# A hybrid eight-layer network on one Trainium2 core: one product for values and sums in the head attention, sums, shifts and router moved into neighbouring stages, random-feature results taken one trip later

## The reference

```python
    x = x + _L0_attn_a_ref(_layernorm(x, axis=-1), ...)
    x = x + _L0_ffn_ref(_layernorm(x, axis=-1), ...)
    x = x + _L0_attn_b_ref(_layernorm(x, axis=-1), ...)
    x = x + _L0_ffn_ref(_layernorm(x, axis=-1), ...)
    x = x + _L1_attn_a_ref(_layernorm(x, axis=-1), ...)
    x = x + _L1_ffn_ref(_layernorm(x, axis=-1), ...)
    x = x + _L1_attn_b_ref(_layernorm(x, axis=-1), ...)
    x = x + _L1_ffn_ref(_layernorm(x, axis=-1), ...)
```

```python
        scores = jnp.einsum('bhid,bhjd->bhij', q, k) * scale
        attn = jax.nn.softmax(scores, axis=-1)
        out = jnp.einsum('bhij,bhjd->bhid', attn, v)
```

```python
            t1, t2 = jnp.split(t, 2, axis=-1)
            t2 = jnp.pad(t2, ((0, 0), (1, 0), (0, 0)))[:, :-1]
            return jnp.concatenate([t1, t2], axis=-1)
```

## Time and profile before

| | us |
|---|---|
| median of 3 runs | 6315.28 |
| lowest, highest run | 6312.53, 6316.73 |
| the profiled execution, as timed | 6308.24 |
| its span in the trace | 6306.2 |

### The profile page before, as it was taken

How to read it: one execution, slowest core, us unless ns; L and a number is a source line. 1 busy time by engine, 2 the same in 40 slices (tenths; PEclk the granted TensorE clock), 3 DMA queues, 4 the chain that set the end, 5 groups by cost and what they waited for, 6 DMA issues and landing times. The chain is left out here.

```text
span 6306.2 us, 119595 instructions
## 1 busy us (share of the span) xinstructions
PE 5418.4 (86%) x42357; PEld 2908.8 (46%) x42357; DVE 3589.7 (57%) x4103; ACT 3331.1 (53%) x4993; POOL 2512.4 (40%) x1721
## 2 busy tenths in 40 slices
PE   6876888888887998998898998999897999776998
PEld 2432555555544553564344554554343444343443
DVE  4557999999954554554344554554454343554344
ACT  4555888888854553554444554454343333443343
POOL 1223999999933651652122661662221000000000
PEclk8996999999998999999899999999899999998999
DMA  1002111101011110110000110110000210001121
GB/s 41 1 0 77 31 32 30 33 30 33 29 47 29 40 40 14 41 41 13 1 0 18 45 40 12 42 40 20 28 0 8 54 40 13 0 0 27 32 36 27
DMA packets 136966, 171.03 MB, mean 27 GB/s; under 512 B 32352, under 2 KB 85728, under 8 KB 135520
## 3 DMA queue, kind: packets, MB, share of 16 engines
q1 hardware_dynamic: 136800, 168.85, 10.2%
HBM read 80.11 MB, written 12.85 MB: 15 GB/s over the span
## 5 line engine op out<-in xcount | busy, mean ns | idle before, releaser
L2318 POOL TENSOR_TENSOR arena<-arena,wbig 128x1024 f32<-128x1024 f32 x512 | 1191.8, 2515 | 103.5 <-DMA wbig<-scratch_b 100.3
L2305 DVE TENSOR_TENSOR_SCAN arena<-banks,arena 128x1024 f32<-128x1024 f32 x512 | 1141.5, 2279 | 63.7 <-ACT banks L2249 45.5
L944 ACT ACTIVATE arena<-banks,wbig 128x512 f32<-128x512 f32 x512 | 352.0, 688 | 584.3 <-PE banks L907 572.7
L601 DVE TENSOR_REDUCE arena<-banks 128x4 f32<-128x1024 f32 (+1 forms) x384 | 401.9, 1047 | 432.8 <-PE banks L435 305.1
L957 DVE TENSOR_TENSOR arena<-arena 128x512 f32<-128x512 f32 x512 | 353.3, 692 | 490.2 <-ACT arena L944 434.7
L768 POOL TENSOR_TENSOR X<-X,Z 128x1536 f32<-128x1536 f32 x2 | 9.5, 4758 | 1482.6 <-ACTq L761 1482.6
L1462 POOL TENSOR_TENSOR arena<-arena 128x512 f32<-128x512 f32 x256 | 355.5, 1389 | 594.5 <-DMA arena<-arena 594.5
L2249 ACT ACTIVATE banks<-banks 128x1020 f32<-128x1020 f32 x512 | 518.2, 1012 | 104.3 <-PE banks L2170 96.8
L2254 ACT COPY arena<-banks 128x1024 f32<-128x1024 f32 x512 | 520.8, 1017 | 51.4 <-POOL arena L2318 30.8
L547 ACT ACTIVATE Y<-banks 128x2048 f32<-128x2048 f32 x192 | 305.8, 1593 | 408.4 <-PE banks L471 311.4
L907 PE MATMUL banks<-Z,wbig 128*128 x1024 | 462.2, 597 | 34.3 <-ACTq L56 34.3
(11 more groups left out here) (289 smaller groups left out, 10428.3 us busy)
## 6 DMA issues: line engine op xcount, KB each, us to landing
arena<-arena SPq DMA_DIRECT2D x1024, 64.0 KB, 2.0
arena<-scratch_g SPq DMA_DIRECT2D x32, 1024.0 KB, 13.8
wbig<-scratch_d SPq DMA_DIRECT2D x512, 16.0 KB, 1.7
wbig<-scratch_b SPq DMA_DIRECT2D x64, 128.0 KB, 2.2
wbig<-scratch_c SPq DMA_DIRECT2D x64, 128.0 KB, 2.1
arena<-Z SPq DMA_DIRECT2D x64, 128.0 KB, 2.1
wbig<-in_l_ffn SPq DMA_DIRECT2D x1, 4197.0 KB, 12.9
X<-in_x SPq DMA_DIRECT2D x2, 2048.0 KB, 14.7
```

The source lines that it names most:

```text
L601: dve.tensor_reduce(to, mbank[:, :, :, 0:keys], AX_X, ALU.max).then_inc(dve_m.sem, 1)
L944: act.activation(hid[e % 2][:, f, :], hbank[f], ACT.Relu, bias=b1[:, e, f:f + 1])\
L2305: dve.tensor_tensor_scan(own, line(decay_bank[n % 2]), own, 0.0, ALU.mult, ALU.add)\
L2318: pool.tensor_tensor(four(h[par][:, m * 1024:m * 1024 + 1024]), four(us[n % 2]), Bs[par].unsqueeze(1).to_broadcast([128, 4, SEQ]), ALU.mult)\
```

## The change

**Head attention.** The values of a slot now stand beside eight columns of ones in `vm`, so that one product gives value rows and sum rows; slots are told apart by column half and by which half of `obank` they go to. L488 and its 128x32 weights are gone. As sums now lie eight partitions below their values, DVE copies the whole bank to `raw`, ACT takes logarithm and exponential over 128x512 (with a scale and a bias that make value rows 1), SP moves the reciprocals up by eight partitions with one transfer, and DVE multiplies twice 128x256 into two arrays, of which the output stage takes two products. `qb` and `km` have two buffers. The addition of the values' bias is gone: a small stage puts it through the output weights once.

```diff
                     pe.wait_ge(pool_s.sem, pool_s.at(i, "vm"))
-                    pe.wait_ge(dve_o.sem, dve_o.before(i, last_out))
+                    pe.wait_ge(dve_o.sem, dve_o.at(i, "raw"))
                 for u in range(2):
                     j = 2 * jj + u
                     for g in range(4):
-                        pe.matmul(obank[rows(g), first:SEQ], vm[par][:, c, j, rows(g)], prob[s % 2][:, g, u, first:SEQ],
-                                  start=(s == 0 and u == 0), stop=True, skip_group_check=True)
-                    for g in range(4):
-                        last = pe.matmul(obank[rows(g), SEQ + first:2 * SEQ], k.c["slot_ones"][:, rows(j)],
-                                         prob[s % 2][:, g, u, first:SEQ], start=False, stop=True,
+                        last = pe.matmul(obank[rows(g), jj * SEQ + first:(jj + 1) * SEQ], vm[par][:, c, j, rows(g)],
+                                         prob[s % 2][:, g, u, first:SEQ], start=(s == 0 and u == 0), stop=True,
                                          skip_group_check=True)
                 last.then_inc(pe_s.sem, 1)
...
+            def logarithm(b):
+                act.wait_ge(dve_o.sem, dve_o.at(b + 1, "raw"))
+                act.wait_ge(dve_o.sem, dve_o.at(b, "out"))
+                act.activation(recip, raw, ACT.Ln, scale=k.c["sum_row"], bias=k.c["head_row"]).then_inc(act_s.sem, 1)
+
             def reciprocal(b):
-                act.wait_ge(pe_s.sem, pe_s.at(b + 1, "late"))
-                act.wait_ge(dve_o.sem, dve_o.before(b, "out"))
-                act.activation(recip, obank[:, SEQ:2 * SEQ], ACT.Ln).then_inc(act_s.sem, 1)
                 act.wait_ge(act_s.sem, act_s.at(b + 1, "ln"))
                 act.activation(recip, recip, ACT.Exp, scale=-1.0).then_inc(act_s.sem, 1)
...
+            def heads_raw(b):
+                dve.wait_ge(pe_s.sem, pe_s.at(b + 1, "late"))
+                dve.wait_ge(dve_o.sem, dve_o.at(b, "out"))
+                dve.tensor_copy(raw, obank).then_inc(dve_o.sem, 1)
+
             def heads_out(b):
-                dve.wait_ge(act_s.sem, act_s.at(b + 1, "recip"))
-                to = out[:, bass.ds(b * SEQ, SEQ)]
-                dve.tensor_tensor(to, obank[:, 0:SEQ], recip, ALU.mult).then_inc(dve_o.sem, 1)
-                if bv is not None:
-                    dve.wait_ge(dve_o.sem, dve_o.at(b, "out"))
-                    dve.tensor_scalar(to, to, bv, None, ALU.add).then_inc(dve_o.sem, 1)
-
+                dve.wait_ge(moved.sem, moved.at(b * 16 + 16))
+                for jj in range(2):
+                    part = slice(jj * SEQ, (jj + 1) * SEQ)
+                    last = dve.tensor_tensor(outs[jj][:, bass.ds(b * SEQ, SEQ)], raw[:, part], moved_to[:, part],
+                                             ALU.mult)
+                last.then_inc(dve_o.sem, 1)
...
+            def trip(b, more):
+                if more:
+                    reduce(b + 1, 0)
+                heads_raw(b - 1)
+                if more:
+                    for n in range(1, 8):
+                        reduce(b + 1, n)
+                heads_out(b - 1)
...
+            def trip(b, par, first=False):
+                keys, queries = kk[:, bass.ds(b * SEQ, SEQ)], q[:, bass.ds(b * SEQ, SEQ)]
+                if not first:
+                    pool.wait_ge(pe_m.sem, pe_m.before(b - 1, "m7"))
+                pool.tensor_copy(qb[par], queries).then_inc(pool_s.sem, 1)
+                pool.tensor_tensor(km[par], spread(keys), mask, ALU.mult).then_inc(pool_s.sem, 1)
+                pool.wait_ge(pe_s.sem, pe_s.before(b, "late"))
...
+        @block.sync
+        def _(sp):
+            for b in range(BATCH):
+                sp.wait_ge(act_s.sem, act_s.at(b + 1, "recip"))
+                sp.wait_ge(dve_o.sem, dve_o.at(b, "out"))
+                sp.dma_start(moved_to[0:128 - HEAD_DIM, :], recip[HEAD_DIM:128, :]).then_inc(moved.sem, 16)
```

```diff
+                if dst is add_to:
+                    dve_s.skip(dve, i, "both")
+                else:
+                    dve.tensor_tensor(dst[:, tok(i, TILE)], dst[:, tok(i, TILE)], add_to[:, tok(i, TILE)], ALU.add)\
+                        .then_inc(dve_s.sem, 1)
...
+        if shifted is not None:
+            @block.gpsimd
+            def _(pool):
+                for i in range(TILES):
+                    pool.wait_ge(dve_s.sem, dve_s.at(i, "sum"))
+                    for to, own in shifted_parts(shifted, dst, i * TILE, TILE):
+                        pool.tensor_copy(to, own)
```

```diff
+            def shift_sum(b):
+                pool.wait_ge(dve_y.sem, dve_y.at(b, "sum"))
+                for to, own in shifted_parts(shifted, y, b * SEQ, SEQ):
+                    pool.tensor_copy(to, own).then_inc(pool_h.sem, 1)
```

```diff
+                        if first and u == 0 and e == 2:
+                            act.wait_ge(chain.sem, chain.at(16))
+                            act.activation(ex_, diff, ACT.Exp).then_inc(weighed.sem, 1)
...
+                        if e % 2 == 0:
+                            dve.wait_ge(landed[u][e // 2].sem, landed[u][e // 2].at(i))
...
+                    for q in quads:
+                        own = slice(q * 2, q * 2 + 2)
                         sp.dma_start(gate[u][:, own, :], k.scratch["g"][own, at:at + TILE].unsqueeze(0)
-                                     .to_broadcast([128, 4, TILE])).then_inc(spread[u].sem, 16)
+                                     .to_broadcast([128, 2, TILE])).then_inc(landed[u][q].sem, 16)
```

```diff
-    pe_s = Steps(k, "products", ["q", "k", "t0", "v", "t1", "h2", "lk0", "nt", "lk1", "n", "mt", "z", "mb", "o", "lq0",
-                                 "lq1"], trips)
-    act_s = Steps(k, "lookups", ["eq0", "copy", "q", "k", "k2", "eq1", "t0", "t1", "ntc", "s1", "ek0", "ln", "rec",
+    pe_s = Steps(k, "products", ["on", "t0", "v", "od", "t1", "h2", "lk0", "nt", "lk1", "n", "q", "k", "z", "mt", "mb",
+                                 "lq0", "lq1"], trips)
+    act_s = Steps(k, "lookups", ["eq0", "copy", "q", "k", "k2", "eq1", "t0", "t1", "ln", "rec", "ntc", "s1", "ek0",
                                  "ek1"], trips)
-    dve_s = Steps(k, "vectors", ["h2", "mk0", "v", "mk1", "mks", "mk", "sums", "m1", "diag", "eps", "s2", "m", "sk0",
-                                 "sk1", "mq0", "sq0", "ctx", "mq1", "sq1"], trips)
...
+            def contexts(to, weight):
+                for b in range(2):
+                    for a in range(4):
+                        last = pe.matmul(to[rows(a), :], weight[:, a, b, :], pT[:, :, 2 * a + b, :],
+                                         start=(weight is num_w and b == 0), stop=True, skip_group_check=True)
+                return last
```

726 lines of the change are left out of this document (425 added, 301 removed).

## The result

| us | before | after |
|---|---|---|
| median of the runs | 6313.9 (4 runs) | 6118.5 (4 runs) |
| lowest, highest | 6310.6, 6316.7 | 6117.3, 6125.0 |
| the profiled execution, as timed | 6308.2 | 6125.0 |
| its span | 6306.2 | 6123.2 |

The ratio is 0.969, with a 95% interval of 0.968 to 0.971: 195 us less, where 175 were forecast (6140; the range of 6095 to 6205 holds the result). By the two spans it is 183 us. The 12 us between these belong to no stage: the profiled execution of before lay 6 us under its median, that of after 6 over. The medians further down are of runs at the usual granted clock of about 0.95; one run of `k1_one_output` at 0.63, which took 7661 us, is left out.

The account below looks back on a forecast made before the run. No single engine bounds the whole: serial stages follow one another, PE's list and waits bounding head attention. Attention -87, shifts and sums -57.6, router -18.4, random features -13 sum to -176; 6315.3 less that is 6139, given as 6140, range 6095 to 6205.

Parts of the forecast that it names:

- Head attention, loop: Three head attentions: trips of 14.5 us unmasked and 15.7 masked, 127 us gained over fifteen trips each.
- the buffers' share: Head attention: second qb and km remove PE's wait for km, 1.36 us a trip unmasked, 1.07 masked.
- the products' share: Head attention: products with ones removed, 3.44 us of PE's list a trip unmasked, 2.58 masked, partly hidden by next bounds.
- L609's share: Third head attention: the bias addition of 1.70 us goes, so 3.15 us a trip less instead of the second's 2.2.
- Ends: Start and end of each head attention: +1.2 us for POOL's memsets, +5.3 for the last batch's longer ending.
- Output stages: After each head attention: 16 more instructions, +5.2 us, plus 1.1 for a cold clock.
- Shifts and sums: Eight shift stages -34.2 us, five sums -32.2, copies and small additions moved elsewhere; net -57.6, bounds -50 and -61.
- The covers: POOL's shifted copies hide behind other work in windowed attention; uncovered, 0.8 us a trip in four stages costs 51 us.
- Mixture: Router with experts: first gate waits 5.2 us instead of 14.4, transfers issued at the same time; -18.4, bounds -14 and -22.
- Random features: Steady trips +5 us with 14 clock dips, start -7, ending -10, padding's stage -0.9; net -13, bounds -25 and 0.
- The port: Rival (0.17, with chains): DVE's heads_out multiplications stand still behind POOL's work, up to 1.9 us a trip; 85 us, 6225.
- the clock: Rival (0.05): TensorE's clock falls to 1.2 GHz in the attention loops as PE's list thins; +377 instead of -127, 6644.

Follow-up runs that it names:

- k1_one_output: Kernel after, with the two column halves of a batch's heads joined into one array, so the output stage has one product a tile; 6104.9 us.
- f2_gates_first: Kernel after, with ACT's router exponential ahead of the second expert's relus and the first gates' transfer issued ahead of four transfers into Y; 6113.0 us.
- h1_longer_pool: Kernel after, with six more POOL multiplications of 128x768 behind km in each trip, meant to run during DVE's multiplications in heads_out; 6140.5 us.
- n1_all: Kernel after with maskless looks, joined heads, earlier router exponential and gates, later raw, reordered random features with five unread products; 6019.5 us, 0.953 of the kernel before.

## Why the prediction came out as it did

**Head attention, loop: right in sum, wrong in the split.** Trips of 14.25 and 15.68 for 14.5 and 15.7. But the buffers' share was put at 1.36 and 1.07 and is 1.08 and 0.7; the products' share was thereby put at 1.74 and 1.13 and is 2.25 and 1.5. The two errors cancel, and that is luck. Without a mask the buffers' error is the wait of 0.25 for DVE that stood behind the one for `km`. With one it is a misreading: the waits of the whole stage were divided by 16 trips, and some 7 of the 17.1 us belong to the stage's start. The 3.0 of PE's waits without a mask are the same misreading; ten steady trips show 20.9 us, 2.1 a trip, so PE's list was to come to 12.1 and not 11.1 (by the trace after it is 12.4). It bound nothing there. L609's share (0.98 forecast, 0.97 in the kernel before with two buffers) was right. Of the next bounds, PE's list with a mask was named rightly. Without one both chains were named, the exponentials 0.1 ahead; the look chain binds, at 14.25 for 14.3, and the exponentials' chain lies at 13.9 to 14.0 for 14.4. The transfer hides in the loop as forecast: `heads_out` waits for it in the last two batches of each attention alone.

**Ends.** Forecast +1.2 at the start and +5.3 at the end of each. From the stage's first instruction to the first exponential it is 21.1, 23.5 and 23.2 us before and 21.4, 23.7 and 24.0 after, so the start costs 1.5 in all three for 3.6 forecast; from the last exponential to the end it is 3.7, 3.7 and 4.1 before and 7.6, 7.2 and 7.2 after, so +3.5. The transfer landed 3.1 us after the start of its issue (3.2 forecast), and the 0.7 for the issue that the sum adds is already in that; the last values, too, have half of their products, 0.86 us, which the step did not take off. Start and end together are some 7.5 us of the 12 to 13 by which the attentions gained more than forecast; the trips are 4.4.

**Output stages.** +22.3 for +18.9: the second product costs 17.9 by `k1_one_output` (15.6 forecast), the clock the rest.

**Shifts and sums: right in sum**, 58 for 57.6, which is closer than the stages in that row repeat. The thirteen stages that are gone took 71.0 us from the start of each to the start of the next (66.4 forecast); the MLPs grew by 7.0 and the windowed attentions by 4. The row also holds 3.8 us by which the state-space scan, which the change leaves alone, was longer in the trace after. The covers held. A gain was overlooked: PE idles in a shift or a sum, and the norm behind it began at a lower granted clock. One norm behind a shift before, and the same norm after:

```profile
2383.13:2405.05 21.92, 17.42 (x32) 0.87 0.00 0
```

```profile
2331.30:2350.32 19.02, 14.52 (x32) 1.00 0.00 1
```

The norms behind the first sum and behind four of the shifts took 108.2 us in all before, at 0.86 to 0.90, and 97.7 after, at 0.92 to 1.00.

**Mixture: the step that failed.** The first gate comes 5.55 us after its transfer is issued, close to the 5.2 forecast. But "the gates' transfers are issued [at the same time] in both versions" was wrong: the router now takes 22.3 us from its first product to that issue, where it took 20.3. ACT's exponential stands behind relus that nobody needs yet (1.3 us, by `f2_gates_first`); the other 0.7 is the router's own products, 3.43 us for 2.70, beside a granted clock of 0.59 for 0.63 in the stage's first 4 us. A step moved into another engine's list had been costed at nothing without reading what is queued ahead of it.

**Random features: right in sum, by two errors that cancel.** -13.1 for -13. The steady trips were to cost 5 us more and cost 1: a trip at the full clock is 19.31 (-0.27; -0.1 forecast; the detour of `eps` is 0.41, not 0.6), and 13 of the 15 trips after have a dip, some of them two (14 forecast), so that the mean trip went from 20.52 to 20.59. The start and the end gave 14 for 18. What I had not seen is how much the clock decides in this stage: a shorter chain did not help while PE was left idle around it.

**Rivals.** The port is real, as `h1_longer_pool` shows, and the clock fell in some trips there. Neither struck here: POOL is done in time, and PE's waits in the loops are short (the loops stand at 1.00). One argument against the clock was misread, though: the random features did not keep 1.00 "in most trips" even before. 11 of the 16 trips had a dip, and the prediction's own count from the earlier trace rows was 9 or 10. The Trainium skill ("TensorE: Matmul & The Clock Gate", What's actually happening) has the throttled state as the default and activity as what releases it; `n1_all`, with the idle gaps filled, agrees. The clock decided nothing in the attention loops, where I had weighed it, and 20 us in the random features.

The forecast's median was 21 us too high: 7 by the sum of the stages, and the rest because I added the 7 us by which the profiled execution of before lay below its median, while the one of after lay above. The scatter of single executions goes both ways and is no term of a sum.

## What to carry to other kernels

- Read a wait in the steady trips, not as a stage's sum over its trips: 17.1 us in the stage's row was 0.65 a trip and some 7 at the start. Then read how far behind the next limit stands: the exponentials' chain was 0.3 us behind the look chain without a mask and 1.45 behind PE's list with one, and of a wait of 1.33 us 1.08 were gained.
- When a step moves into a stage that is already running, read what is queued ahead of it on its new engine and what its completion starts; ordering the first transfer ahead of less urgent ones gave 2.2 us a stage, and a small step ahead of unneeded ones 1.3.
- Where a chain of tiny steps leaves TensorE idle once a trip, look at the granted clock there before shortening the chain. Here products that nobody reads, in the gaps and off the chain, were worth 20 us, and 0.41 us off the chain nothing.

## What was not expected of the hardware

- With TensorE's gaps of 0.67, 0.63 and 1.5 us filled, the granted clock of the random features' steady trips went from 0.90 to 1.00 and the trip from 20.6 to 19.17 us; with only the last one filled it was 0.93 and 20.5, each on top of the other order.
- DVE's 128x256 multiplication with two SBUF inputs took 0.42 us alone; with POOL's 1.47 us multiplications about, single ones took up to 1.69, the two of a trip 0.71 and 1.05 on average; its reductions from PSUM kept their 1.22 beside the same POOL work.
- A transfer of 240 KB within SBUF landed 3.1 us after issue, 48 times of 48 within 3.1 to 3.4, and a first one of 512 KB from DRAM, spread to 128 partitions, after 5.5.
